# Throttling the gather engine of a graph network by its own drain instead of by landed gathers

## The reference

```python
# L0: four graph convolutions, widths 128 -> 256 -> 256 -> 256 -> 128
h = x @ W
msg = h[src] * norm[:, None]
out = jax.ops.segment_sum(msg, dst, num_segments=n_nodes) + b
# after the first three: * sigmoid(a), layernorm, elu
...
# L1: two graph attention layers, 8 heads of 16, on the nodes' 128 values
att = jnp.clip(jnp.einsum('ehd,ehd->eh', q[dst], k[src]) / scale, -50, 50)
alpha = exp(att - segment_max(att)[dst]) / segment_sum(exp(...))[dst]
aggr = jax.ops.segment_sum(v[src] * alpha, dst, num_segments=n)
x = x + aggr @ Wo + bo
x = x + gelu(layernorm(x) @ W1 + b1) @ W2 + b2
...
# around each network: x = layernorm(x + network(x))
```

## Time and profile before

| | us |
|---|---|
| median of 3 runs | 7774.36 |
| the three runs | 7771.58, 7774.36, 8287.29 |
| profiled execution, its own time | 7761.23 |
| its span, first to last instruction | 7759.4 |
| mean granted TensorE clock, share of full speed | 0.791 |

### The profile page before, as it was taken

How to read it: one execution, slowest core, us unless ns; L and a number is a source line. 1 busy time by engine, 2 the same in 40 slices (tenths; PEclk the granted TensorE clock), 3 DMA queues, 4 the chain that set the end, 5 groups by cost and what they waited for, 6 DMA issues and landing times.

```text
span 7759.4 us, 116895 instructions
## 1 busy us (share of the span) xinstructions
PE 5133.9 (66%) x25317; PEld 3898.4 (50%) x25540; DVE 3876.6 (50%) x10619; ACT 677.3 (9%) x1598; POOL 3351.6 (43%) x3512
## 2 busy tenths in 40 slices
PE   2677556765788667886566555666777655666666
PEld 1122455654566556665445444455666444555555
DVE  8544355652333323343334445556666545566665
ACT  0011000000000000000000100011112100111111
POOL 0000455545444454443555454455554254545542
PEclk9955666777899878997677677788888777888887
DMA  1011322332333333333222233333333233333331
GB/s 43 33 50 66 104 77 77 99 90 76 108 121 112 95 89 100 103 99 101 74 78 80 73 101 100 99 101 104 104 103 99 66 103 98 101 101 104 101 95 55
DMA packets 308017, 695.49 MB, mean 90 GB/s; under 512 B 68843, under 2 KB 118116, under 8 KB 306526
## 3 DMA queue, kind: packets, MB, share of 16 engines
q0 software_dynamic: 146944, 381.90, 17.5%
q10 hardware_dynamic: 94612, 196.31, 7.4%
q1 hardware_dynamic: 66250, 114.82, 5.0%
HBM read 624.93 MB, written 67.83 MB: 89 GB/s over the span
## 4 chain that ended last, share of the span: by engine, by line
DMA 33%; issue 25%; PE 18%; POOL 9%; DVE 9%; DVEq 3%; ACT 1%; POOLq 1%; SPq 0%; ACTq 0%
DMA ring<-rows,idx_stage 32%; POOL ring L1391 9%; PE acc_ps L1835 5%; PE acc_ps L1853 2%; PE acc_ps L1787 1%; PE q_ps L1777 1%; PE acc_ps L1747 1%; PE q_ps L1747 1%; DVE even_rows L582 1%; PE acc_ps L1748 1%; PE bank L1889 1%; PE q_ps L1748 1%; DVE masks L808 1%; DVE dots L993 1%; PE bank L2028 1%
## 5 line engine op out<-in xcount | busy, mean ns | idle before, releaser
L1391 POOL DMA_INDIRECT ring<-rows,idx_stage x3360 | 3312.1, 986 | 3247.2 <-DMA ring<-rows,idx_stage 1846.4
L1853 PE MATMUL acc_ps<-ring,masks 128*128 x4800 | 1226.3, 419 | 954.5 <-SPq L1304 587.7
L1853 PEld LDWEIGHTS acc_ps<-ring,masks 128*128 128x128 f32 x4800 | 975.2, 253 | 1171.6 <-issue 1082.7
L1777 PE MATMUL q_ps<-odd_rows,conv_only 128*128 (+1 forms) x3904 | 766.6, 365 | 951.3 <-DVE conv_only L796 871.5
L788 DVE SCALAR_TENSOR_TENSOR masks<-dst_f,neg_first,lane 128x256 f32<-128x256 f32 x1200 | 548.7, 483 | 1334.9 <-PE acc_ps L1853 1012.0
L1777 PEld LDWEIGHTS q_ps<-odd_rows,conv_only 128*128 128x128 f32 x3904 | 675.7, 264 | 1026.5 <-issue 1022.5
L1787 PE MATMUL acc_ps<-msg,masks 128*128 x3904 | 644.9, 316 | 156.7 <-DVE msg L1005 142.0
L1787 PEld LDWEIGHTS acc_ps<-msg,masks 128*128 128x128 f32 x3904 | 601.3, 224 | 279.0 <-issue 267.3
L796 DVE TENSOR_SCALAR conv_only<-conv_only,node_id 128x512 f32 x488 | 240.5, 493 | 727.2 <-SPq L1333 553.6
L1376 POOL COPY idx_stage<-src_idx 128x28 int32 (+1 forms) x126 | 33.3, 265 | 1060.4 <-DVE turn_b L729 810.4
L808 DVE SCALAR_TENSOR_TENSOR masks<-dst_f,neg_first,lane 128x512 f32<-128x512 f32 x488 | 366.9, 752 | 236.6 <-PE acc_ps L1787 197.9
(11 more groups left out here) (278 smaller groups left out, 6240.6 us busy)
## 6 DMA issues: line engine op xcount, KB each, us to landing
conv_only<-dst_rows SPq DMA_DIRECT2D x394, 256.0 KB
ring<-rows,idx_stage POOLq DMA_INDIRECT x3360
adjacency<-odd_rows ACTq DMA_DIRECT2D x10, 3136.0 KB, 8.9
conv_only<-adjacency ACTq DMA_DIRECT2D x70, 384.0 KB
msg<-adjacency ACTq DMA_DIRECT2D x60, 384.0 KB
wide<-adjacency ACTq DMA_DIRECT2D x60, 384.0 KB
turn_b<-adjacency ACTq DMA_DIRECT2D x60, 384.0 KB
part<-adjacency ACTq DMA_DIRECT2D x30, 448.0 KB
```

The lines of the kernel that those rows point to most:

```text
L1391: pool.indirect_dma_start(ring[:, j, 0:WIDTH[p]], None, tables[p][:, :], bass.IndirectOffsetOnAxis(ap=idx_stage[:, half, j:j + 1], axis=0) ...
L1777: ins = pe.matmul(to, mask_t[:, u, j, :], q_rows[:, bass.ds(t + u, 1), :].rearrange("p a f -> p (a f)"), start=u == 0, stop=u == nxt)
L1853: ins = pe.matmul(to, masks[:, u, j, :], rhs, start=False, stop=final and j == GC - 1)
```

## The change

POOL no longer waits, before gather j of a lap, for the landing of gather j - 2. Instead it executes a drain after every second gather (j odd). All other waits are as before: on the freed group, on the staged indices, and SP's wait for all four landings of a group.

```diff
                     for j in range(q * GC, (q + 1) * GC):
-                        if j >= 2:
-                            pool.wait_ge(landed[j - 2], lap * 16 + 16)
-                            pool.sem_inc(slots_seen, 1)
                         pool.indirect_dma_start(
                             ring[:, j, 0:WIDTH[p]], None, tables[p][:, :],
                             bass.IndirectOffsetOnAxis(ap=idx_stage[:, half, j:j + 1], axis=0),
                         ).then_inc(landed[j], 16)
+                        if j % 2 == 1:
+                            pool.drain()
                     if q == RG // 2:
```

## The result

The changed kernel takes 9669.32 us (median of 4 runs, 9656.6 to 9686.2) against 7772.97 us before: 1.245 times as long, 95% interval 1.2434 to 1.2466. The prediction said 6925 us. The profiled execution has a span of 9654.5 us against 7759.4.

A forecast was written before the change was run, and what follows sets the result against it. Gather latency and the limit of two in flight were taken to bound the kernel. Per-pass savings of 1067 us, 80% kept as 850, took the profiled 7761 us to 6911, plus 13 for the median: 6925 us, range 6580 to 7420.

The forecast's parts named there:

- The bound now: POOL's gathers: held by latency and the limit of two in flight, not bandwidth; some 4 us a pair.
- the 3.93 us from start to landing: Gather's start to its landing, read from the chain in one small stretch, then 0.76 us until the waiting gather starts.
- Up to 28 gathers ahead of the landings: POOL without landing waits: may run that far ahead of the landings, as far as freed groups let it.
- Removed: POOL's landing waits: 3120 waits and 3120 semaphore increments go; their instructions cost nothing that shows, the waiting goes.
- The sum's rule: Each pass takes the larger of its gathers' time and its users' time, the present length less waits for landed groups.
- cheap drain: Rival: the drain hides in the 0.30 us between gathers, all 1137 us of starvation are saved; 6640 us, chance 22%.
- Added: POOL: 1680 drains, one behind each pair, 0.8 us from pair's end to next pair; bounds zero to about 1.2 us.
- 0.76 and a little: POOL's gap from a pair's end to the next pair: 0.76 us plus a little for the drain, taken as 0.8 us.
- The rival "slower": POOL's drain ends only when both gathers have landed: 5.95 us a pair, 10500 us; chance 10%, milder forms included.
- The port pair: VectorE's lock on the port shared with GpSimd may lengthen gathers; if the 141 us doubled, some 60 us longer.
- A gap of 3 us and more behind each pair would be the slower case: Sign in POOL's profile: such a gap means the drain waits for landings; the forecast had about 0.8 us.
- the waits for landed groups: Sign: engines' waits for landed groups, 1137 us in all before, go down to a fifth; attention passes near 1330 us.

The follow-up runs named there:

- e6: Kernel before the change with the landing wait three or one gathers back instead of two: 7766 us with three, 13209 us with one.
- e1: Changed kernel with its drains removed, so neither landing waits nor drains: 6754 us on chip 1, ratio 0.871 to the kernel before.
- e5: Kernel before the change with the landing wait four or eight gathers back instead of two: 6767 and 6768 us on chip 2.
- e8: Kernel before the change without landing waits, one drain behind the 28th gather of each lap, 120 in all: 6893 us on chip 2.
- e2: Changed kernel with the drain behind each second gather replaced by explicit waits for both gathers' landings: 9650 us, ratio 1.244 to the kernel before.
- e3: Changed kernel with waits for both gathers' landings put before each pair's drain: 9947 us, ratio 1.282 to the kernel before.
- e7: Changed kernel, drains kept, with gathers of 128 bytes a row instead of 512 or 1024 and the ring's other columns zeroed once: 9070 us, one run.

## Why the prediction was wrong, step by step

**The bound now: right.** Gathers' latency and the limit of two held the kernel. e6 with one back and e1, e5 and e8 on chips 1 and 2 move the time as that says. One number was misread: the 3.93 us from start to landing is a slow one; the median is 2.8 us in every run with whole rows whose trace shows it. "Up to 28 gathers ahead of the landings" was too wide as well: at most 7 were in flight at once (e1).

**Removed: right on two chips, wrong on three.** Without the waits and without drains the time is 6754 us on chip 1. The sum's rule (users' time without starvation, gathers at 1.29 us) had all 1137 us saved under "cheap drain"; against that chip's own 7752 us it is 998 us, 12% less. On chip 5 the same kernel gains nothing (8004 us), and waits three or four back gain nothing on chips 3 and 4. If the chip of the result was one of these, as its missing records suggest, a cheap drain would not have brought 6925 us there either. No row that the prediction used told of those stalls, and a premise went unexamined: that more gathers in flight touch nobody else.

**Added: the step that failed.** "The upper end is a drain that costs its own 0.26 and a second turn of the sequencer, about 1.2 us." The gap behind a pair is 2.8 us in the median of the attention passes, where the sum had 0.8 us. The bound was taken from a drain behind a memset, which leaves nothing in flight. The drain's own price was even well read (0.198 us against 0.26), but what it waits for wasn't. The bound needed the landing in it: the drain ends 0.11 us after the second gather has landed, and the next gather starts 0.73 us after that, the "0.76 and a little" of the prediction, but counted from the landing.

**The rival "slower": the mechanism was right, at 10%.** It had the pair at 1.29 + 3.9 + 0.76 = 5.95 us and the time at 10500 us. Measured: 5.12 us and 9669 us, and with the median landing of 2.8 us its own sum gives 4.85 us. With means it closes: 1.25 us to the second gather's start, 2.87 to its landing, 0.11 to the drain's end, and 0.73 (inside a group) or 1.13 (at a group's start) to the next gather are 5.16 us. What was said against it was a wrong inference: the index copy behind a gather starts at once while the gather is in flight. That shows that POOL takes new work then, not that a drain would count the gather as done. The sentence of the Trainium skill beside it ("PSUM — Partial Sum Buffer", section "Engine vs sequencer instructions": a drain waits for the engine to go fully idle) holds by its wide reading: on POOL, idle includes the transfers in flight (e2, e3, e7).

**The port pair** of the Trainium skill's page "SBUF — State Buffer", section "SBUF: two separate sides", had no visible part in the result: the gather's mean is 965 ns in the changed kernel and 994 ns in e1 against 986 before, so that no doubling of the 42 ns came.

**The signs named beforehand.** "A gap of 3 us and more behind each pair would be the slower case": the profile shows 2.8 us, just under it and far from the 0.8 us of the forecast. POOL's waits for landings are gone as foretold, but the waits for landed groups grew instead of falling to a fifth, and an attention pass takes 2008 us, not 1330.

Why is waiting for both landings so much worse than waiting for the one two back, with two in flight in either case? With the rolling wait the next gather goes out 0.76 us after the first one's landing, while the second is still on its way: 3.56 us a pair at best. The drain waits for the second one, which started 1.25 us later, and keeps nothing in flight across the gap: 1.25 + 2.8 + 0.8 = 4.85 us.

## What to carry to other kernels

On POOL a drain behind an indirect DMA that it has issued is a wait for the landing, whatever semaphore the kernel leaves out; price it with the landing, not with a drain that finds nothing in flight. A rolling wait n transfers back should be free once n times the time to hand one out is longer than the landing and the restart: on chips 1 and 2 that held for four (5.0 against 3.56 us), and for three (3.75 us) it was never seen. A barrier on all of them costs a landing each time that the ring doesn't cover. A gain from more transfers in flight has to be seen on several chips before it is believed: here the same kernel was 13% faster on one and 3% slower on another.

## What the runs showed of the hardware

- A drain on POOL behind indirect gathers ended 0.11 to 0.13 us after the last one's landing, in all 1680 pairs of the changed kernel (median 3.86 us in the sequencer for a landing of 2.8 us); with nothing in flight it took 0.198 us (e3), and behind 28 gathers it ended 1.18 us after the last landing (e8).
- A gather of 128 rows landed 2.8 us after its start in the median, 2.4 us with 128 bytes a row. With up to 7 in flight (e1) the median was 2.81 us and the mean 3.08, with at most two on the same chip (e2) 2.76 and 2.92 us.
- With the wait three or more back, or none, three of five chips showed 14 to 20% of the chain under a releaser that the profile can't name: VectorE and ScalarE waited for signals of TensorE that are on record over 1.5 us after its instruction's end (0.02 us at most on chips 1 and 2). With the wait one or two back it was 13 us at most in the whole span. The cause is open.
